# ScalarE's planes split first and its norms moved to the end of a convolution step, with a transposition issued ahead of weight loads

## The chip, the core and the metric

The kernel runs on one core of a Trainium2 chip. The metric is the device time of one execution in microseconds (us), the median of several runs. A core has five engines that run side by side and meet only at semaphores: TensorE (PE, matrix products), VectorE (DVE), ScalarE (ACT), GpSimd (POOL) and SyncE (SP), which here issues almost all DMAs.

## The reference

The program is two gated layers over x (8 batches, 256 rows, 512 columns) with a context of the same shape. The change touches only the first part of it:

```
x = x + tanh(g_xattn[0]) * _L0_xattn_ref(ctx, ctx, _layernorm(x), ssm_kernel, D, 8)
x = x + tanh(g_ffn[0])   * _L0_ffn_ref(_layernorm(x), w1, w2, w3)
x = x + tanh(g_xattn[1]) * _L1_xattn_ref(_layernorm(x), ctx, mask)
x = x + tanh(g_ffn[1])   * _L1_ffn_ref(_layernorm(x), w1, w2, w3)
```

`_L0_xattn_ref` takes, in each of 32 heads of 8 rows, all products of context row i with context row j, convolves each of them along the 512 columns with the head's own kernel (plus D times the product), multiplies with row i of the normed x and sums over i:

```
kv  = einsum('bhil,bhjl->bijhl', k, v)
out = irfft(rfft(kv) * rfft(ssm_kernel))[..., :L] + kv * D
out = einsum('bijhl,bhil->bjhl', out, q)        # q = layernorm(x)
```

## The kernel before

x lies in 16 tiles of 128 rows by 512 columns; a tile n holds two heads of all eight batches. The convolution runs in 16 steps, n = 0 to 15, each of two heads (hh = 0, 1). It is written as products with Toeplitz blocks. Every engine has its own loop over n, written out by hand, and the order inside a loop is the order of the code; nothing is planned by a scheduler. A step is made of these parts:

- GpSimd: `pairs(n + 1)` multiplies context rows (L583, L586); `finish_heads` closes the sum over i (L600, L603); `ln_root(n + 3)` and `conv_offset(n + 3)` make the scale and the offset of the norm of x's tile n + 3 from VectorE's sums (L296, L302, L591); `add_result(n - 2)` adds the finished step n - 2 to x (L607).
- TensorE: `conv_head(n, 0)` and `conv_head(n, 1)`, 36 float32 products each, 72 records in the trace (L740). Between the two stands `turn_result(n - 2)` (L732), which transposes a finished result into a PSUM bank. That bank is also one of the banks of `conv_head(n, 1)`. So in the middle of that head, after 21 of its 36 products, TensorE waits on `s_re`, for ScalarE to have copied the result away. `conv(n)` begins only when `pairs(n)` (`s_kv`), the squares (`s_sq`) and its Toeplitz block have come.
- VectorE: `products(n, hh)` reads the convolution from PSUM and multiplies it with the normed x (L1334, L1336, L1338, L1343), `fold_heads` (L1349) adds, `ln_sums(n + 3)` makes the sums of x's tile n + 3 (L287, L289).
- ScalarE: the path of the normed x, the squares of the context (`square`, L1097), the copy of the result (`copy_result(n - 2)`, L1114), and work on the first feed-forward's weights, `sum_weight` (L1118) and `ternary` (L1125, L1128).

The normed x has a path of its own from tile 2 on. `norm_q(n)` (L1105, two instructions) writes the normed tile into `xh_c`; it waits for GpSimd's offset (`s_off`). `split_q(n)` (L1070, two) takes the float32 words apart into two planes of 16-bit halves in `q_planes`. SyncE's `turn_q_planes(n)` (L378) is a DMA transposition of both planes into `qT_planes`. `join_q(n)` (L1081, four) puts the halves together again for VectorE. `q_planes` and `qT_planes` exist once: `split_q(n + 1)` waits until transposition n has landed, and transposition n + 1 waits until `join_q(n)` is done (`s_qc`) and `split_q(n + 1)` is done (`s_xh`).

SyncE's queue is one row of DMAs and waits in the order of the code: in a step x's tile n + 4, the context of step n + 2, weight chunks of the first feed-forward (two chunks of 704 KB in steps 0 to 3, one in steps 5 to 8; L384), the transposition, and the Toeplitz block of step n + 2 (L366). A wait holds all that stands behind it.

Of the kernel before, what the change touches and what calls it, by code (L numbers as in the profile page):

```python
# [24 lines left out]
def at(v, off, dims):  # L25
    return bass.AP(v.tensor, v.offset + off, [v.ap[0]] + dims)


def flamingo_two_layers(nc, xc, cx, ctxt_in, ctx_in, mask, g_xattn, g_ffn, taps_in, dskip, a_w, b_w, out):
    NT = xc.shape[0]  # L30
# [35 lines left out]
    with ExitStack() as ctx:  # L66
# [276 lines left out]
        def chunk_of(v, j, size):  # L343
            return v[:, j * size:(j + 1) * size]

        with nc.Block() as block:
            @block.sync
            def _(sp):
                def load_context(n):
                    if n >= 2:  # L350
                        sp.wait_ge(s_kv, n)
                        if n == 2:
                            sp.wait_ge(s_first, 3)
                        sp.wait_ge(s_sq, n)
                    sp.dma_start(cx_sb[n % 2], cx[n]).then_inc(s_cx[n % 2], 16)

                def load_x(n):
                    sp.dma_start(x_sb[:, n, :], xc[n]).then_inc(s_xl[n], 16)

                def load_toeplitz(n):  # L360
                    if n >= 2:
                        sp.wait_ge(s_y, 2 * n - 2)
                    if n == 2:
                        sp.wait_ge(s_kpad, 16)
                    rows = (kpad if n >= 2 else taps_in)[n * G:n * G + G, :]
                    sp.dma_start(toep[n % 2], bass.AP(rows.tensor, rows.offset, [[1, P], [TAP, G], [1, L]])  # L366
                                 ).then_inc(s_tp[n % 2], 16)
# [6 lines left out]
                def turn_q_planes(n):  # L374
                    sp.wait_ge(s_xt, 2 + 16 * (n - 2))
                    sp.wait_ge(s_xh, 2 * n)
                    sp.wait_ge(s_qc, n)
                    sp.dma_start_transpose(qT_planes, q_planes).then_inc(s_xt, 16)  # L378

                def load_weight(w, j):  # L380
                    if w == 2:
                        sp.wait_ge(s_wr, j + 1)
                        sp.wait_ge(s_ws, j + 1)
                    sp.dma_start(chunk_of(w_in[w % 2], j, AC), a_w[w][:, j * AC:(j + 1) * AC]).then_inc(s_w[w][j // 2], 16)  # L384

                def turn_x(t):
                    sp.wait_ge(f_qi, t + 1)
                    if t >= 4:
                        sp.wait_ge(f_up, 3 * (t - 4) + 3)
                    sp.dma_start_transpose(fa_qT[t % 4], fa_qi[t % 2]).then_inc(f_xT[t % 4], 16)  # L390
# [18 lines left out]
                def load_b(j):  # L409
                    home = B_HOME[j]  # L410
                    if j == 0:
                        sp.wait_ge(s_wr, 8)
                        sp.wait_ge(s_ws, 8)
                    if j == 5:
                        sp.wait_ge(s_xh, 2 * NT - 2)
                    if j == 6:
                        sp.wait_ge(s_rt, NT)
                        sp.wait_ge(s_prod, 2 * NT)
                    if home >= 8:
                        sp.wait_ge(c_m, NT)  # L420
                    elif home in B_HOME[:j]:
                        sp.wait_ge(s_ba, max(q for q in range(j) if B_HOME[q] == home) + 1)
                    sp.dma_start(b_in[home], b_w[j // PERW][:, (j % PERW) * BCH:(j % PERW + 1) * BCH]
                                 ).then_inc(s_b[home % 8], 16)
# [25 lines left out]
                for n in range(NT):  # L450
                    if n + 4 < NT:
                        load_x(n + 4)
                    if n + 2 < NT:
                        load_context(n + 2)
                    for w, first in ((0, 0), (1, 2)):
                        if n in (first, first + 1):
                            load_weight(w, 2 * (n - first))
                            load_weight(w, 2 * (n - first) + 1)
                    if 5 <= n < 9:
                        load_weight(2, n - 5)  # L460
                    if n == 0:
                        sp.wait_ge(s_dadd, 1)
                        sp.dma_start(kpad[:, :], kp_sb).then_inc(s_kpad, 16)
                    if n + 2 < NT:
                        turn_q_planes(n + 2)
                        load_toeplitz(n + 2)
                    if n in B_EARLY:
                        load_b(B_EARLY[n])
                    if n == 15:
                        sp.wait_ge(s_qc, NT)  # L470
                        sp.dma_start(mask_u8, mask.rearrange("b c -> (b c)").rearrange("(a n) -> a n", a=1)
                                     .to_broadcast([P, B * C])).then_inc(s_gate, 16)
                    if n >= NT - 2:
                        turn_x(n + 2 - NT)
# [579 lines left out]
            def _(act):  # L1054
# [9 lines left out]
                def split_q(n):  # L1064
                    act.wait_ge(s_xh, 2 * n - 1)
                    if n >= 3:
                        act.wait_ge(s_xt, 2 + 16 * (n - 2))
                    src = xh_c[n % 2].bitcast(U16)
                    for half in range(2):
                        last = nc.scalar.activation(q_planes[:, half * L:(half + 1) * L], at(src, half, [[2, L]]), ACT.Copy)  # L1070
                    last.then_inc(s_xh, 1)
# [28 lines left out]
                def norm_q(n):  # L1100
                    act.wait_ge(s_off, n + 1)
                    if 2 <= n < 4:
                        act.wait_ge(s_xt, n - 1)
                    for first, swap in ((0, Q), (P + Q, -Q)):
                        last = nc.scalar.activation(at(xh_c[n % 2], first - first % P, [[2 * P, 2], [Q, 2], [1, Q]]),  # L1105
                                                    at(x_sb[:, n, :], first, [[2 * P, 2], [swap, 2], [1, Q]]), ACT.Identity,
                                                    bias=ln_off[:, n:n + 1], scale=ln_rs[:, 0, n:n + 1])
                    last.then_inc(s_xh, 1)

                def copy_result(n, bk):  # L1110
                    act.wait_ge(s_rt, n + 1)
                    if n >= 2:
                        act.wait_ge(s_r0, n - 1)
                    nc.scalar.activation(rt[n % 2], bank(bk), ACT.Copy, scale=gates[:, 0:1]).then_inc(s_re, 1)  # L1114
# [6 lines left out]
                def ternary(w, j):  # L1121
                    if j == 0:
                        act.wait_ge(s_mean, 2 * w + 2)
                    src = chunk_of(w_in[w % 2], j, AC)
                    nc.scalar.activation(src, src, ACT.Identity, bias=magic[:, 0:1], scale=a_inv[:, w:w + 1]  # L1125
                                         ).then_inc(s_wr, 1)
                    act.wait_ge(s_wr, 4 * w + j + 1)
                    nc.scalar.activation(chunk_of(a_flat[w], j, AC), src, ACT.Sign, bias=magic[:, 1:2]).then_inc(s_ws, 1)  # L1128
# [83 lines left out]
                for n in range(NT):  # L1212
                    if n == 2:
                        act.wait_ge(s_kpad, 16)
                    if n == 0:
                        copy_q(1)
                    elif n + 1 < NT:
                        join_q(n + 1)
                    if n + 1 < NT:
                        square(n + 1)  # L1220
                    if n + 2 < NT:
                        norm_q(n + 2)
                        split_q(n + 2)
                    if n == 0:
                        act.wait_ge(s_gate, 32)
                        nc.scalar.activation(gates[:, :], gates[:, :], ACT.Tanh).then_inc(s_tanh, 1)
                        act.wait_ge(s_tanh, 1)
                        act.wait_ge(s_const, 6)
                    if n >= 2:
                        copy_result(n - 2, 4)  # L1230
                    for w in range(3):
                        for j in range(4):
                            if ABS_STEP[w, j] == n:
                                sum_weight(w, j)
                            if TERN_STEP[w, j] == n:
                                ternary(w, j)
                    if NT - 3 <= n < NT - 1:
                        a_round_x(n + 3 - NT)

# [520 lines left out]
```

## Time and profile before

| | us |
|---|---|
| median of 3 runs | 692.6 (692.45 to 693.28) |
| the profiled execution, its own time | 695.11 |
| its span in the trace | 693.3 |
| PE busy | 678.9 (98%) |
| DVE busy | 582.7 (84%) |
| ACT busy | 414.9 (60%) |
| POOL busy | 295.0 (43%) |

The convolution takes about the first 173 us of the span; then come the first feed-forward, the attention and the second feed-forward. In the chain of work that ended last, GpSimd holds 15% of the span, VectorE 6% and TensorE 68%. GpSimd's part lies in the convolution; from 178.87 us on the chain consists almost only of TensorE's products. Busy shares are averages over these stages, so a change in the convolution has to be read inside the convolution.

### The profile page before, as it was taken

The page shows a single profiled execution, that of the slowest core. Times are in us where ns is not written, and L with a number is a line of the kernel's source. Part 1 is how long each engine was busy: PE and PEld are TensorE (multiplying, and loading weights), DVE is VectorE, ACT ScalarE, POOL GpSimd, SP SyncE. Part 2 cuts the span into 40 slices and gives each one's busy share as a digit, 9 for nine tenths or more (in the row PEclk, how much of TensorE's full clock was granted, in tenths as well). Part 3 has the DMA queues.
Part 4 walks back from the last instruction along what each step waited for, and adds up shares of the span by engine and source line. Part 5 has one row for each costly group of instructions (what it writes and reads, how often), then busy time and mean ns, then how long its engine had stood idle before and what let it go on. Part 6 is the DMA issues. An engine that isn't in the chain of part 4 may idle for free.

```text
span 693.3 us, 12921 instructions
## 1 busy us (share of the span) xinstructions
PE 678.9 (98%) x4826; PEld 357.8 (52%) x4826; DVE 582.7 (84%) x1054; ACT 414.9 (60%) x646; POOL 295.0 (43%) x455
## 2 busy tenths in 40 slices
PE   9989999999999999999999999999999999999997
PEld 6756555555444444567754444444444444444445
DVE  5979999998998998658958889988888888898891
ACT  3689999856679989748667444434434434434440
POOL 6869999999765544537400521111110111110000
PEclk9999999999999999999999999999999999999999
DMA  8797775553379789998042243363332334342234
GB/s 296 222 293 209 227 188 141 148 148 111 102 167 194 187 167 201 218 357 308 17 136 17 61 94 75 91 92 92 76 90 41 68 92 92 77 78 59 61 71 112
DMA packets 155390, 94.85 MB, mean 137 GB/s; under 512 B 133825, under 2 KB 134337, under 8 KB 155329
## 3 DMA queue, kind: packets, MB, share of 16 engines
q1 hardware_dynamic: 153600, 90.02, 51.8%
q0 software_dynamic: 1200, 3.93, 1.7%
q8 instruction: 38, 0.62, 0.4%
q14 instruction: 24, 0.19, 0.1%
q10 hardware_dynamic: 528, 0.09, 0.1%
HBM read 53.04 MB, written 8.47 MB: 89 GB/s over the span
## 4 chain that ended last, share of the span: by engine, by line
PE 68%; POOL 15%; DVE 6%; issue 3%; ACT 2%; DMA 1%; SPq 0%; POOLq 0%; ACTq 0%
PE psum L955 29%; PE psum L987 15%; PE psum L882 9%; POOL phase_space L583 5%; PE psum L894 4%; PE psum L938 4%; PE psum L916 4%; POOL phase_space L600 3%; POOL x_sb L607 2%; POOL phase_space L586 2%; POOL phase_space L603 1%; PE psum L740 1%; PE psum L971 1%; DMA x_sb<-x_between 1%; POOL ln_rs L302 1%
## 5 line engine op out<-in xcount | busy, mean ns | idle before, releaser
L955 PE MATMUL psum<-phase_space 128*128 128x512 f16 x1024 | 223.8, 379 | 0.1
L955 PEld LDWEIGHTS psum<-phase_space 128*128 128x128 f16 x1024 | 100.0, 98 | 122.2 <-issue 1.7
L740 PE MATMUL psum<-phase_space 64*64 64x288 f32 x2304 | 150.3, 409 | 6.3 <-POOL phase_space L586 3.5
L740 PEld LDWEIGHTS psum<-phase_space 64*64 64x64 f32 x2304 | 89.9, 134 | 61.0 <-POOL phase_space L586 8.5
L712 POOL DMA_DIRECT2D out<-x_sb x15 | 9.3, 621 | 234.6 <-DVE x_sb L1516 234.6
L987 PE MATMUL psum<-phase_space 128*128 128x512 f16 x480 | 105.7, 379 | 0.0
L1281 ACT ACTIVATE phase_space<-psum,b_scalars 128x512 f32<-128x512 f32 x64 | 43.4, 682 | 75.2 <-PE psum L955 75.1
L1287 ACT ACTIVATE phase_space<-phase_space,magic 128x1024 f32<-128x1024 f32 x32 | 36.4, 1148 | 77.3 <-DVE phase_space L1500 77.3
L882 PE MATMUL psum<-phase_space 128*128 128x512 bf16 (+1 forms) x384 | 78.8, 361 | 0.7 <-DVE phase_space L1343 0.7
L987 PEld LDWEIGHTS psum<-phase_space 128*128 128x128 f16 x480 | 47.0, 98 | 56.6
L1485 DVE SCALAR_TENSOR_TENSOR phase_space<-psum,b_scalars,phase_space 128x512 f32<-128x512 f32 x64 | 47.7, 748 | 28.4 <-ACT phase_space L1281 28.3
L882 PEld LDWEIGHTS psum<-phase_space 128*128 128x128 bf16 x384 | 37.4, 98 | 40.9 <-issue 0.8
L583 POOL TENSOR_TENSOR phase_space<-phase_space 128x512 f32<-128x512 f32 x45 | 48.2, 1097 | 0.0
L1440 DVE TENSOR_REDUCE phase_space<-phase_space 128x8 f32<-128x512 f32 (+1 forms) x32 | 47.4, 1480 | 0.6
L287 DVE BATCH_NORM_STATS2 ln_bn<-x_sb 128x6 f32<-128x512 f32 x64 | 43.5, 680 | 3.0 <-DMA x_sb<-x_between 2.6
L1334 DVE TENSOR_TENSOR phase_space<-psum,phase_space 128x1024 f32<-128x1024 f32 x32 | 39.0, 1220 | 5.6 <-PE psum L740 4.9
L307 POOL TENSOR_SCALAR phase_space<-x_sb,ln_nm,ln_rs 128x512 f32<-128x512 f32 x48 | 38.0, 791 | 12.4 <-POOL ln_rs L302 5.8
L894 PE MATMUL psum<-phase_space 128*128 128x512 bf16 x176 | 40.6, 379 | 1.0 <-issue 0.6
L1147 ACT ACTIVATE phase_space<-psum,a_scalars 128x512 f32<-128x512 f32 (+1 forms) x48 | 30.8, 642 | 14.4 <-PE psum L882 13.1
L314 POOL TENSOR_TENSOR phase_space<-phase_space 128x512 f16<-128x512 f32 x12 | 13.8, 1179 | 59.4 <-ACT phase_space L1293 59.4
L1507 DVE SCALAR_TENSOR_TENSOR phase_space<-phase_space 128x1024 f32<-128x1024 f32 x32 | 37.8, 1223 | 1.3
L1382 DVE SCALAR_TENSOR_TENSOR phase_space<-psum,a_scalars,phase_space 128x512 f32<-128x512 f32 (+1 forms) x48 | 33.2, 696 | 5.9 <-ACT phase_space L1147 4.9
(123 smaller groups left out, 1081.7 us busy)
## 6 DMA issues: line engine op xcount, KB each, us to landing
phase_space<-in_L_weights SPq DMA_DIRECT2D x24, 512.0 KB, 6.0
phase_space<-in_L_weights SPq DMA_DIRECT2D x12, 704.0 KB, 7.1
phase_space<-kpad SPq DMA_DIRECT2D x14, 512.0 KB, 4.3
phase_space<-in_context_heads SPq DMA_DIRECT2D x15, 384.0 KB, 5.2
x_sb<-in_x_tiles SPq DMA_DIRECT2D x16, 256.0 KB, 4.8
phase_space<-in_context_turned SPq DMA_DIRECT2D x8, 512.0 KB, 5.9
x_between<-x_sb SPq DMA_DIRECT2D x16, 256.0 KB
x_sb<-x_between SPq DMA_DIRECT2D x16, 256.0 KB, 6.8
```

Source lines behind the costliest of these rows:

```text
L287: nc.vector.bn_stats(ln_bn[:, stage, n % 2, :], x_sb[:, n, :]).then_inc(s_ln[stage], 1)
L307: nc.gpsimd.tensor_scalar(dst, x_sb[:, n, :], ln_nm[:, stage, n:n + 1], ln_rs[:, stage, n:n + 1], ALU.add, ALU.mult).then_inc(s_done, 1)
L583: nc.gpsimd.tensor_tensor(at(kv_k, d * E, [[NP, rows], [1, E]]), at(cx_sb[k], 0, [[EX, rows], [1, E]]), at(cx_sb[k], d, [[EX, rows], [1, E ...
L740: return nc.tensor.matmul(at(dst, 0, [[64, B], [1, NP]]), toep[n % 2][row:row + Q, hh, shift:shift + Q], kv[n % 2][row:row + Q, IN_SLOT[j] ...
L882: last = nc.tensor.matmul(bank(UPA[c][part])[:, 0:w], fa_qT[t % 4][:, kk, :], a_wT[part][:, kk, c0:c0 + w], start=(kk == 0), stop=(kk == L ...
L894: last = nc.tensor.matmul(bank(6 + t % 2), fa_hT[t % 2][:, c, :], a_wT[2][:, c, :], start=(c == 0), stop=(c == JA - 1))
L955: last = nc.tensor.matmul(bank(2 * (m % 3) + w), fb_qT[n % 2][:, kk % 2, kk // 2, :], b_wT[w][:, kk // 2, c * 512:(c + 1) * 512], start=(k ...
L987: last = nc.tensor.matmul(bank(6 + k), fb_hT[k][:, part, c, :], b_wT[2][:, c, :], start=(c == 0 and part == 0), stop=(c == JB - 1 and part ...
L1281: nc.scalar.activation(fb_s[m % 2], bank(2 * (m % 3)), ACT.Silu, scale=fb_sm[:, n % 4, 2:3]).then_inc(g_si, 1)
L1334: nc.vector.tensor_tensor(at(pr, 0, [[SLOTS, rows], [E, 4], [1, E]]), at(y, 0, [[64, rows], [1, 32]]), at(q, 0, [[EX, rows], [1, 4], [1, E ...
L1440: nc.vector.tensor_reduce(gx[:, 0, :], grouped(src), AX.X, ALU.max, apply_absolute_value=True).then_inc(s_steps, 1)
L1485: nc.vector.scalar_tensor_tensor(fb_h[n % 2][:, c * 512:(c + 1) * 512], bank(2 * (m % 3) + 1), fb_sm[:, n % 4, 3:4], fb_s[m % 2], ALU.mult ...
```

## The change

ScalarE's step is put in another order. Before, in a step n it did `join_q(n + 1)`, `square(n + 1)`, `norm_q(n + 2)`, `split_q(n + 2)`, `copy_result(n - 2)`, and then the weights. Now it does `split_q(n + 2)`, `join_q(n + 1)`, `square(n + 1)`, `copy_result(n - 2)`, the weights, and `norm_q(n + 3)` last. Step 0 keeps its order and has `norm_q(3)` added at its end. SyncE issues the transposition of a step ahead of that step's weight chunks, from step 1 on, and no longer behind them.

```
@@ SyncE
                     if n + 2 < NT:
                         load_context(n + 2)
+                    if 1 <= n < NT - 2:
+                        turn_q_planes(n + 2)
                     for w, first in ((0, 0), (1, 2)):
                         if n in (first, first + 1):
                             load_weight(w, 2 * (n - first))
@@
                     if n == 0:
                         sp.wait_ge(s_dadd, 1)
                         sp.dma_start(kpad[:, :], kp_sb).then_inc(s_kpad, 16)
+                        turn_q_planes(2)
                     if n + 2 < NT:
-                        turn_q_planes(n + 2)
                         load_toeplitz(n + 2)
@@ ScalarE
                     if n == 2:
                         act.wait_ge(s_kpad, 16)
+                    if 1 <= n < NT - 2:
+                        split_q(n + 2)
                     if n == 0:
                         copy_q(1)
                     elif n + 1 < NT:
                         join_q(n + 1)
                     if n + 1 < NT:
                         square(n + 1)
-                    if n + 2 < NT:
-                        norm_q(n + 2)
-                        split_q(n + 2)
+                    if n == 0:
+                        norm_q(2)
+                        split_q(2)
@@
                             if TERN_STEP[w, j] == n:
                                 ternary(w, j)
+                    if n + 3 < NT:
+                        norm_q(n + 3)
                     if NT - 3 <= n < NT - 1:
                         a_round_x(n + 3 - NT)
```

No instruction is added or removed. In the changed file the lines of ScalarE stand two lines lower (L1105 is L1107, L1114 is L1116, and so on; the tanh of the gates, L1226, is L1230).

Here is ScalarE before, from the weight sums of step 1 (L1118) to the copy of the first result in step 2 (L1114):

```order
L1118 ACTIVATE phase_space,a_abs<-phase_space 128x1408 x2
L1081 ACTIVATE phase_space<-phase_space 128x64x8
L1081 ACTIVATE phase_space<-phase_space 128x64x4
L1081 ACTIVATE phase_space<-phase_space 128x64x8
L1081 ACTIVATE phase_space<-phase_space 128x64x4
L1097 ACTIVATE phase_space<-phase_space 128x64x8
L1105 ACTIVATE phase_space<-x_sb,ln_off,ln_rs 128x2x128 x2
L1070 ACTIVATE phase_space<-phase_space 128x512 x2
L1114 ACTIVATE phase_space<-psum,gates 128x512
```

And the same place of ScalarE now, from the weight sums of step 1 (L1120) to the same copy (L1116):

```order
L1120 ACTIVATE phase_space,a_abs<-phase_space 128x1408 x2
L1107 ACTIVATE phase_space<-x_sb,ln_off,ln_rs 128x2x128 x2
L1072 ACTIVATE phase_space<-phase_space 128x512 x2
L1083 ACTIVATE phase_space<-phase_space 128x64x8
L1083 ACTIVATE phase_space<-phase_space 128x64x4
L1083 ACTIVATE phase_space<-phase_space 128x64x8
L1083 ACTIVATE phase_space<-phase_space 128x64x4
L1099 ACTIVATE phase_space<-phase_space 128x64x8
L1116 ACTIVATE phase_space<-psum,gates 128x512
```

The norm and the split of tile 4 stood behind the join of tile 3 and the square; now they stand ahead of them. What stands between the weight sums and the copy is the same work.

On SyncE's queue this is the difference in step 1, with the transposition (L378), the two weight chunks (L384) and the Toeplitz block (L366):

```order
 L355 DMA phase_space<-in_context_heads 128x768
+L378 DMA_TRANSPOSE phase_space<-phase_space 128x8x128
 L384 DMA phase_space<-in_L_weights 128x1408 x2
-L378 DMA_TRANSPOSE phase_space<-phase_space 128x8x128
 L366 DMA phase_space<-kpad 128x2x512
```

The transposition has moved up past the two chunks, so the chunks now stand behind its waits. The Toeplitz block is behind all three, as it was.

## Rows read from the trace of the kernel before

**Rows 1.** Windows of 20 us: start:end, length, busy us and count per engine, clock, DMA.

```profile
20.00:40.00 20.00, 17.48 (x262) 12.21 (x258) 17.66 (x24) 14.55 (x26) 18.57 (x25) 0.94 0.98 294
...
100.00:120.00 20.00, 19.02 (x296) 11.24 (x292) 19.39 (x25) 18.91 (x28) 19.14 (x24) 1.00 0.56 142
```

**Rows 2.** Chain that ended last, whole span: start, us, engine and line.

```profile
38.20 7.99 PE psum L740 x102
...
55.66 3.57 POOL phase_space L583 x3
...
147.79 3.11 POOL phase_space L583 x3
```

**Rows 3.** Timeline of PE, convolution: start, us, line, count, [idle before, releaser].

```profile
15.69 16.31 PE L740 MATMUL psum<-phase_space 64*64 64x288 f32 x264
...
32.82 3.12 PE L740 MATMUL psum<-phase_space 64*64 64x288 f32 x42
38.20 7.99 PE L740 MATMUL psum<-phase_space 64*64 64x288 f32 x102 [2.26 <-ACT phase_space L1114]
...
160.84 6.69 PE L740 MATMUL psum<-phase_space 64*64 64x288 f32 x102 [0.52 <-ACT phase_space L1114]
```

**Rows 4.** Window of 2 us behind TensorE's long wait, columns as in rows 1.

```profile
38.00:40.00 2.00, 1.80 (x16) 1.05 (x20) 0.01 (x1) 2.00 (x4) 1.72 (x4) 0.50 1.18 374
```

**Rows 5.** Timelines of DVE and of POOL, steps 2 and 3.

```profile
41.89 1.22 DVE L1334 TENSOR_TENSOR phase_space<-psum,phase_space 128x1024 f32<-128x1024 f32 x1 [3.88 <-PE psum L740]
...
29.82 0.27 POOL L591 TENSOR_SCALAR ln_off<-ln_ag,ln_rs 128x1 f32<-128x1 f32 x1
...
47.25 0.73 POOL L603 TENSOR_TENSOR phase_space<-phase_space 128x256 f32<-128x256 f32 x1
51.76 0.19 POOL L296 TENSOR_SCALAR ln_ve<-ln_ag 128x1 f32<-128x1 f32 x1 [3.77 <-DVE ln_ag L289]
```

**Rows 6.** Timeline of ACT, from the first join to the first copy.

```profile
24.29 2.11 ACT L1081 ACTIVATE phase_space<-phase_space 128x512 uint16<-128x512 uint16 x4 [4.85 <-DMA phase_space<-phase_space]
26.26 0.61 ACT L1097 ACTIVATE phase_space<-phase_space 128x512 f32<-128x512 f32 x1
...
27.89 1.15 ACT L1070 ACTIVATE phase_space<-phase_space 128x512 uint16<-128x512 uint16 x2
...
32.85 2.08 ACT L1081 ACTIVATE phase_space<-phase_space 128x512 uint16<-128x512 uint16 x4 [1.10 <-issue]
...
37.48 0.67 ACT L1114 ACTIVATE phase_space<-psum,gates 128x512 f32<-128x512 f32 x1
```

**Rows 7.** Timeline of SP's queue, step 1: start of issue and its length.

```profile
23.61 0.90 SPq L384 DMA_DIRECT2D phase_space<-in_L_weights  x2
29.10 1.24 SPq L378 DMA_TRANSPOSE phase_space<-phase_space  x1
```

**Rows 8.** Transpositions (L378): those issued at 37.63, then at 57.80, to landing.

```profile
DMA to landing us min/median/max: 5.5/5.5/5.5
...
DMA to landing us min/median/max: 2.8/2.8/2.8
```

**Rows 9.** Weight chunks (L384), all twelve issues of the convolution, to landing.

```profile
DMA to landing us min/median/max: 5.1/7.1/9.9
```

**Rows 10.** Timelines of POOL, ACT, PE and DVE within one later step.

```profile
93.39 0.27 POOL L591 TENSOR_SCALAR ln_off<-ln_ag,ln_rs 128x1 f32<-128x1 f32 x1
...
102.66 0.19 POOL L296 TENSOR_SCALAR ln_ve<-ln_ag 128x1 f32<-128x1 f32 x1
...
93.69 1.09 ACT L1105 ACTIVATE phase_space<-x_sb,ln_off,ln_rs 128x256 f32<-128x256 f32 x2 [0.32 <-POOL ln_off L591]
...
96.03 4.59 PE L740 MATMUL psum<-phase_space 64*64 64x288 f32 x72
101.12 4.59 PE L740 MATMUL psum<-phase_space 64*64 64x288 f32 x72 [0.49 <-POOL phase_space L586]
...
101.22 1.23 DVE L1334 TENSOR_TENSOR phase_space<-psum,phase_space 128x1024 f32<-128x1024 f32 x1
```

More of the change, by code:

```diff
@@ L454, in _ @@
                         load_context(n + 2)
+                    if 1 <= n < NT - 2:
+                        turn_q_planes(n + 2)
                     for w, first in ((0, 0), (1, 2)):
@@ L463, in _ @@
                         sp.dma_start(kpad[:, :], kp_sb).then_inc(s_kpad, 16)
+                        turn_q_planes(2)
                     if n + 2 < NT:
-                        turn_q_planes(n + 2)
                         load_toeplitz(n + 2)
@@ L1214, in _ @@
                         act.wait_ge(s_kpad, 16)
+                    if 1 <= n < NT - 2:
+                        split_q(n + 2)
                     if n == 0:
@@ L1220, in _ @@
                         square(n + 1)
-                    if n + 2 < NT:
-                        norm_q(n + 2)
-                        split_q(n + 2)
+                    if n == 0:
+                        norm_q(2)
+                        split_q(2)
                     if n == 0:
@@ L1236, in _ @@
                                 ternary(w, j)
+                    if n + 3 < NT:
+                        norm_q(n + 3)
                     if NT - 3 <= n < NT - 1:
```

## The prediction, made before the changed kernel was run

> **What bounds the kernel now.** I read the chain of waits first, since busy shares mix the stages. Inside the convolution it has two parts. Up to 55.66 us it passes from ScalarE to TensorE, VectorE and GpSimd; from there on it is GpSimd alone, step after step [rows 2]. `pairs` starts at 55.66 and, nine steps later, at 147.79: 10.24 us a step. The windows agree: between 100 and 120 us GpSimd is busy 19.14 of 20 us [rows 1]. So from 55.66 us on a change on ScalarE gains nothing unless it changes GpSimd's start; it can only lose something by making GpSimd wait. What can be gained lies ahead of 55.66.
>
> There TensorE's timeline shows the place [rows 3]. In step 2 it does 42 records of `conv_head(2, 1)` from 32.82 on, then sits idle for 2.26 us and resumes at 38.20, released by ScalarE's L1114, which is `copy_result(0)`. That wait costs more than itself. The 102 records behind it take 7.99 us; the same 102 behind a short wait of 0.52 us at 160.84 take 6.69 us [rows 3]. The granted clock is 0.50 between 38 and 40 us, the lower of its two levels (1.2 and not 2.4 GHz), after the idle stretch [rows 4]. VectorE then waits 3.88 us for TensorE, and GpSimd 3.77 us for VectorE's sums of x at 51.76, though its work of that time had ended at 47.98 [rows 5]. All behind that is GpSimd's chain.
>
> **The change part by part.** No instruction comes or goes, so the sum is of times at which `copy_result(0)` ends, and what follows from it. I follow ScalarE from the row at 24.29, where it begins on transposition 2, which landed then [rows 6]. Nothing ahead of that moves but `norm_q(3)`, which goes into step 0: it takes 1.12 us (1.09 of one pair and the gap to the next [rows 10]) and falls in the 4.85 us in which ScalarE waits for that transposition [rows 6].
>
> - `split_q(3)`, now first: 24.29 to 25.35 (1.06 us from a split's start to the next start, 27.89 to 28.95 [rows 6]).
> - `join_q(2)`: 1.97 us (24.29 to 26.26 [rows 6]), to 27.32. `square(2)`: 0.61, ending at 27.93, the next start at 27.83.
> - Transposition 3 may be issued when both are done, at 27.4 instead of 29.10 [rows 7].
> - The two weight sums of step 1: 2.80 us (28.95 to 31.75, where the idle time of the row at 32.85 begins [rows 6]), to 30.63. `norm_q(4)`: its offset is there at 30.09 [rows 5]; to 31.75.
> - `split_q(4)` needs transposition 3 landed. Transpositions took 2.8 and 5.5 us at the ends [rows 8], so it lands between 30.2 and 32.9. I take 3.7, what it took in this place before (29.10 to about 32.8, where ScalarE takes it up [rows 6, 7]): 31.1, before ScalarE needs it. `split_q(4)` to 32.81, `join_q(3)` to 34.76, `square(3)` to 35.27, `copy_result(0)` to 35.94, against 37.48 + 0.67 = 38.15 [rows 6].
>
> The transposition's late end, 5.5 us, would put all this 1.15 us later. It took 5.5 us at 37.63, with weight chunks issued shortly ahead of it, and 2.8 us at 57.80, where the step had no chunks [rows 8]; now no chunk of its own step stands ahead of it. The Trainium skill (DMA: Bandwidth & Descriptors, "Queues, rings and completion order") says that each DMA engine takes up the descriptors of a ring in their order, so what is issued later queues behind. Those two rows agree with it; by that rule the transposition lands near the short end and the 1.15 us are not paid, and the chunks pay instead. Without it the late end stays in my range.
>
> TensorE pays something back in step 2. It ran without a gap from 15.69, 264 records in 16.31 us [rows 3]; of these 48 and 144 belong to steps 0 and 1, so `conv(2)` began at 15.69 + 192 x 0.0618 = 27.56, and it needs `square(2)`, now done at 27.93 and not at 26.87: 0.4 us late. Half of it is lost in the short wait ahead of `turn_result(0)`; the 42 records then end 0.2 us later. At full clock they take 42 x 0.0639 = 2.68 us, so TensorE comes to its wait at 32.82 + 2.68 + 0.2 = 35.7 and resumes at 36.0: a wait of 0.3 us instead of a long one.
>
> The sum: TensorE resumes 38.20 - 36.0 = 2.2 us earlier, and the 102 records behind it take 7.99 - 6.69 = 1.3 us less, at the clock of rows 3. Together 3.5 us. VectorE takes it all, being free at 41.89 - 3.88 = 38.0, about when the head is done. GpSimd's L296 was ready at 47.98; it would start at 51.76 - 3.5 = 48.3 and still waits, so the 3.5 us pass to it whole. The most it could take is 3.77 [rows 5], and 0.6 us more from a wait on VectorE's fold just ahead, as it then starts the step earlier: 4.4 in all.
>
> Does it arrive at the end? From 55.66 on GpSimd's work is unchanged, and 52.2 is where it starts now. The next test is ScalarE in the later steps, where the new order puts `copy_result` behind more work. `norm_q` starts at 93.69, right after GpSimd's offset [rows 10]; now split, join, square and copy follow it, 1.12 + 1.06 + 1.93 + 0.51 + 0.67 = 5.29 us, so the copy ends at 98.98. TensorE wants it after 42 records, at 96.03 + 2.68 = 98.71, and is 0.3 us late in every such step. But it waits 0.49 us for `pairs` at the next step's start anyway [rows 10]: the 0.3 us come out of that. VectorE needs that head at 101.22, and gets it at 100.6 + 0.3. Cost nothing. If that cover were gone, the cost would be 0.3 us in each of some eight steps, 2.4 us. `square` is done at 98.3, ahead of 101.12. The last three steps have ScalarE waiting for VectorE, and take up what is late.
>
> The weight chunks of step 1 move from 23.61 [rows 7] behind the transposition, to about 28.7 and 29.2. They land 5.1 to 9.9 us later [rows 9]; 7.1 gives 36.3. ScalarE wants them at 35.9, and `norm_q(5)` behind them waits for GpSimd until 39.3 anyway. Their sums are done near 39.2, and VectorE needs the total at about 41.6. Cost nothing; beyond a landing at 38.2 they would delay `copy_result(1)`, which TensorE wants at 46.3. The chunks of later steps have a step or more to spare, and the Toeplitz blocks keep their place, since they wait for the convolution's end.
>
> The profiled execution took 695.11 us, with 1.8 us around its span; it would be 691.6. It lies 2.5 above the median, and the 3.5 us are a difference inside it, so from the median: 692.6 - 3.5 = 689.1.
>
> **The rivals.**
>
> A, partial gain: the chunks or the transposition land late. A chunk landing 9.9 us after 29.2 comes at 39.1, `copy_result(1)` ends at 47.2, TensorE waits 0.9 us in step 3: gain 2.6, time 690.0. The transposition at its 5.5 us: the copy ends at 37.1, the wait is 1.4 us, gain 1.1 to 2.4 depending on the clock, 690.2 to 691.5. For it: the DMA share of 0.98 between 20 and 40 us [rows 1]. Against it: both would have to come at or near the longest row.
>
> B, nothing to be measured: the wait shrinks but the clock falls all the same, and the transposition is late too. Gain 1.1 or less, 691.5 to 692.6. Against it: the clock stayed up behind the 0.52 us wait [rows 3].
>
> C, slower: in steps 6 to 13 TensorE now has a wait inside a head, on `copy_result`. If that second gap a step brought the clock down, the 102 records behind would take 1.3 us more, of which 0.2 are covered by what is left of the 0.49: 1.1 in eight steps, 8.8 us, less the 3.5 gained: 697.9. It decides from five such steps on. Against it: TensorE idles no more per step than now, and the window from 100 to 120 us, with a gap of 0.49 a step, has a clock of 1.00 [rows 1, 10]. And a late head alone, with no fall of the clock, reaches GpSimd only over VectorE's sums, which end at 101.3 and are wanted at 102.66 [rows 10]: another 1.3 us to spare.
>
> D, the change does not do what it says: `norm_q(n + 3)` waits for its offset and holds the split, join and square behind it, so the transposition loop runs no earlier. In later steps this is so; there it does not matter. In steps 1 and 2 the offset is there before ScalarE is (30.09 against 30.63). This would give 692.6.
>
> **How the numbers follow.** The forecast 689.1 (gain 3 to 4.4) has a chance of 0.73, A 0.13, B and D together 0.08, C 0.06. What can be told from no change is about 0.2%, 1.4 us. Faster by more: the forecast and A, 0.86; within: 0.08; slower: 0.06. The low end is the most GpSimd can take, 4.4: 688.2. The high end is A's, 691.3; beyond both lie B, D and C.
>
> **What would show it.** Right: TensorE's wait on L1116 in step 2 is under 0.6 us and the clock stays at 1.00 from 34 to 44 us; GpSimd's wait at L296 in step 3 falls from 3.77 to about 0.5 to 1 us (it starts at 48.3); `pairs` starts at 52.2 and again every 10.2 us; in later steps TensorE has small waits on L1116, and those on GpSimd shrink by as much. Wrong: ScalarE's L1072 in step 2 waits for the transposition past 32 us, its L1120 waits for chunks past 38 us, or the step grows beyond 10.24 us, with the clock below 1.00 in 60 to 150 us.

## The result, and the profile after

| | us |
|---|---|
| before, median of 20 runs | 693.12 (692.45 to 693.8) |
| changed, median of 20 runs | 691.48 (691.02 to 692.42) |
| ratio | 0.9977, 95% interval 0.9971 to 0.9984 |
| the profiled executions, before and changed | 695.11 and 691.55 |
| their spans | 693.3 and 689.7 |

The change gains 1.6 us; 3.5 were forecast. Single runs over 1.5% above the fastest of their kernel (two of before and one of a variant, all in the comparisons below) are in no median. The two profiled executions, though, differ by 3.6 us (691.6 was forecast for that of the changed kernel), and their rows differ as the prediction said. This is TensorE's timeline of the changed kernel in steps 2 and 3:

```profile
15.68 11.94 PE L742 MATMUL psum<-phase_space 64*64 64x288 f32 x192
27.89 4.59 PE L742 MATMUL psum<-phase_space 64*64 64x288 f32 x72 [0.27 <-ACT phase_space L1099]
...
33.00 3.12 PE L742 MATMUL psum<-phase_space 64*64 64x288 f32 x42
36.30 6.53 PE L742 MATMUL psum<-phase_space 64*64 64x288 f32 x102 [0.18 <-ACT phase_space L1116]
```

The wait on the copy is 0.18 us where [rows 3] have 2.26, and the 102 records behind it take 6.53 us, not 7.99. `conv(2)` now waits 0.27 us for `square(2)`, which was foreseen. The granted clock in windows of 2 us (columns as in rows 1) stays up where [rows 4] have 0.50:

```profile
36.00:38.00 2.00, 1.82 (x29) 1.13 (x32) 1.93 (x4) 2.00 (x4) 1.73 (x2) 1.00 1.07 382
38.00:40.00 2.00, 2.00 (x39) 1.24 (x34) 1.53 (x3) 1.61 (x4) 1.68 (x4) 1.00 1.09 324
```

GpSimd's timeline, step 3 and the start of step 4, against [rows 2, 5]: its wait for VectorE's sums is 0.38 us and not 3.77, and `pairs` starts at 52.43, 3.2 us earlier.

```profile
48.54 0.19 POOL L296 TENSOR_SCALAR ln_ve<-ln_ag 128x1 f32<-128x1 f32 x1 [0.38 <-DVE ln_ag L289]
...
52.43 3.57 POOL L585 TENSOR_TENSOR phase_space<-phase_space 128x512 f32<-128x512 f32 x3
```

From 62.96 on the chain of waits (start, us, what) has GpSimd's `pairs` once a step, every 10.2 us, as before:

```profile
62.96 3.11 POOL phase_space L585 x3
...
93.54 3.12 POOL phase_space L585 x3
103.73 3.12 POOL phase_space L585 x3
```

So the mechanism is in the profile, and yet half of the time is missing in the median. The place to look is the kernel before.

### The profile page after: what moved, and what is told of

Same layout as the page of the kernel before. It is cut to its first block, busy times and chain, and to the rows that moved or that the text cites. A ratio compares the mean times of both kernels' runs of the same rounds, so it can differ in the third digit from the quotient of the medians.

```text
span 689.7 us, 12909 instructions
## 1 busy us (share of the span) xinstructions
PE 680.3 (99%) x4814; PEld 359.3 (52%) x4826; DVE 582.2 (84%) x1054; ACT 414.2 (60%) x646; POOL 295.1 (43%) x455
## 4 chain that ended last, share of the span: by engine, by line
PE 73%; POOL 15%; DVE 5%; ACT 3%; issue 2%; DMA 2%; POOLq 0%; ACTq 0%; SPq 0%
PE psum L957 29%; PE psum L989 15%; PE psum L884 11%; PE psum L896 5%; POOL phase_space L585 5%; PE psum L940 4%; PE psum L918 4%; POOL phase_space L602 3%; POOL x_sb L609 2%; DMA phase_space<-phase_space 2%; PE psum L742 2%; POOL phase_space L588 2%; POOL phase_space L605 1%; PE psum L973 1%; PE psum L907 1%
## 5 line engine op out<-in xcount | busy, mean ns | idle before, releaser
L742 PE MATMUL psum<-phase_space 64*64 64x288 f32 x2304 | 152.6, 407 | 1.0 <-ACT phase_space L1116 0.6
L742 PEld LDWEIGHTS psum<-phase_space 64*64 64x64 f32 x2304 | 91.4, 133 | 56.5 <-ACT phase_space L1116 4.5
```

Source lines behind the costliest of these rows:

```text
L742: return nc.tensor.matmul(at(dst, 0, [[64, B], [1, NP]]), toep[n % 2][row:row + Q, hh, shift:shift + Q], kv[n % 2][row:row + Q, IN_SLOT[j] ...
```

## Experiments

All ratios are to the kernel before on the same chip, with 95% intervals. Lines of the changed kernel are two higher than those of before. "`pairs` of step 4" is what GpSimd does in its own step 4.

### The kernel before, once more

No edit.

> The kernel before once more, for a second profile and the granted clock of each timed run. The question: the profiled executions differ by 3.6 us (695.11 and 691.55), the medians by 1.64 us (693.12 and 691.48). Theory 1 (the profiled execution of before was not typical: TensorE's wait in step 2 was long enough there to bring the clock down, in most executions it is not, or less so): ratio to before 1.000, the new profiled time lies near 693.1, its wait on L1114 in step 2 is under 2.26 us or its 102 records take less than 7.99 us, and the mean clock of most timed runs is above the 0.997 of that profile. Rival (the wait and the fall of the clock are the same in every execution, and the changed kernel loses some 2 us elsewhere that its profile does not show): the wait is again about 2.26 us, 7.99 us behind it, and the clock of most runs is 0.997.

Measured: ratio 0.9999 (0.999 to 1.0008), median 693.31, profiled execution 692.89 with a span of 691.0. Its TensorE timeline at the same place, and a window of 2 us behind the wait:

```profile
32.82 3.12 PE L740 MATMUL psum<-phase_space 64*64 64x288 f32 x42
37.67 6.53 PE L740 MATMUL psum<-phase_space 64*64 64x288 f32 x102 [1.73 <-ACT phase_space L1114]
```

```profile
38.00:40.00 2.00, 2.00 (x40) 1.28 (x36) 0.11 (x1) 2.00 (x3) 1.73 (x4) 1.00 1.08 280
```

The same program waits 1.73 us here, not 2.26, resumes 0.53 us earlier, and its clock does not fall: 6.53 us for the 102 records. The first join of ScalarE starts 0.54 us earlier, since transposition 2 was issued 0.23 us earlier and landed 4.5 and not 4.8 us after its issue:

```profile
23.75 2.10 ACT L1081 ACTIVATE phase_space<-phase_space 128x512 uint16<-128x512 uint16 x4 [4.54 <-DMA phase_space<-phase_space]
```

Both together are 2.0 us at the end of the 102 records (46.19 against 44.20), of 2.3 us between the two spans. GpSimd's wait on VectorE in step 3 is 2.0 us. Against this profile the changed kernel is 1.37 us earlier at TensorE's resumption (37.67 to 36.30), and its span is 1.3 us shorter: near the measured gain. Theory 1 holds, by this one further profile and by the times of the other runs. That the clock of most runs would lie above 0.997 was right too: the runs list 0.998 to 1.000. A mean of 0.998 or 0.999 is no sign of a fall in step 2, though: in this profile the mean is 0.999 with a clock of 1.00 in step 2, because it is lower at the very end (0.82 from 688 to 690 us, 0.50 behind that), where TensorE has no work left.

Timed runs like the first profile exist, but are few: of 98 runs of before in all comparisons, 9 took 693.9 us or more, up to 695.2. Five of them, at 694.6 to 695.2, have a mean clock of 0.996 to 0.998, as a fall would leave it; the other four, at 693.9 to 694.5, have 1.000 and so no such fall. Of 31 runs of the changed kernel none took more than 692.42. That the clock fell in step 2 in those five is inferred from their time and mean; only profiles show the place.

### Each half alone

SyncE's half, ScalarE as before:

```
+                    if 1 <= n < NT - 2:
+                        turn_q_planes(n + 2)   # ahead of load_weight
...
```

> SyncE's part of the change alone: the transposition issued ahead of the weight chunks, ScalarE in its old order. Transposition 3 still waits for split_q(3), so it is issued near 29.1; ahead of it no chunk of its step. My theory (ScalarE's order is what brings the copy forward): the transposition lands up to 0.9 us earlier, so the wait of 2.26 us shrinks by 0 to 0.9; gain over before 0 to 0.9 us, ratio 0.9987 to 1.000. Rival (the chunks on the queue are what makes it late): the gain is most of the whole change's 1.6 us, ratio 0.9977.

Measured: 0.9989 (0.998 to 0.9998), 692.61 us. ScalarE's half, SyncE as before:

```
+                    if 1 <= n < NT - 2:
+                        split_q(n + 2)         # ahead of join_q(n + 1)
...
+                    if n + 3 < NT:
+                        norm_q(n + 3)          # at the step's end
```

> ScalarE's part of the change alone: split first, norm of the next but one last; SyncE in its old order. My theory: transposition 3 is issued near 27.4 behind chunks that were issued at 23.6; even if it takes 4.8 us it lands at 32.2, so the copy of the first result ends within about 0.5 us of where it ends in the whole change: gain 1.2 to 1.6 us, ratio 0.9977 to 0.9983. Rival (both parts are needed): under half of it, ratio above 0.9988.

Measured: 0.9989 (0.998 to 0.9998), 692.50 us. TensorE's timeline at the place in question, of SyncE's half and then of ScalarE's half:

```profile
37.20 6.53 PE L742 MATMUL psum<-phase_space 64*64 64x288 f32 x102 [1.10 <-ACT phase_space L1116]
```

```profile
36.57 6.53 PE L740 MATMUL psum<-phase_space 64*64 64x288 f32 x102 [0.52 <-ACT phase_space L1114]
```

Against 37.67, SyncE's half resumes 0.47 us earlier and ScalarE's 1.10, where the whole change has 1.37. These three differences are not the edits' alone, since transposition 2, ahead of all that was moved, landed at another time in each profile. ScalarE's first instruction behind it starts at 24.29 and 23.75 us in the two profiles of before, at 23.43 in SyncE's half, 23.41 in ScalarE's half, and 24.16 and 23.69 in the two of the changed kernel. From there to the start of `copy_result(0)` it is 13.2 us in both profiles of before, 13.05 in SyncE's half, 12.44 in ScalarE's half, and 11.4 and 11.2 in the changed kernel. Counted so, SyncE's half brings 0.15 us alone, ScalarE's 0.8, and both together 1.8 to 2.0, more than the sum. What ScalarE's half lacks is in its row of `split_q(4)`, where ScalarE waits for transposition 3:

```profile
32.33 1.15 ACT L1070 ACTIVATE phase_space<-phase_space 128x512 uint16<-128x512 uint16 x2 [1.01 <-DMA phase_space<-phase_space]
```

It was issued at 26.63 us, behind the chunks, and took 5.6 us. In the changed kernel, with the same order on ScalarE and the chunks behind it, it took 4.6 and 4.3, and 2.8 to 4.6 in the four profiles of kernels built on it. In the medians each half gains 0.7 to 0.8 us of the 1.6, with intervals of 0.6 us to each side that do not tell them apart. SyncE's half is where I expected it; ScalarE's half fell short of my 1.2 to 1.6 us, and its 0.9989 is at the rival's edge. So ScalarE's order is what brings the copy forward, and by these profiles it needs SyncE's to bring all of it.

### One copy moved, all else as before

```
+                    if n == 2:
+                        copy_result(0, 4)      # behind square(3), ahead of norm_q(4)
...
-                    if n >= 2:
+                    if n >= 3:
                         copy_result(n - 2, 4)
```

> The kernel before with one thing moved: in step 2 alone, copy_result(0) stands directly behind square(3), ahead of norm_q(4) and split_q(4). The copy then ends near 36.0 instead of 38.15, all else on ScalarE and SyncE as before. My theory (the whole gain is TensorE's wait for this one copy): the same time as the changed kernel, ratio to before 0.9970 to 0.9983, and GpSimd's pairs of step 4 start near 52.4. Rival (the gain comes from the earlier transpositions in all steps): ratio 0.999 to 1.000.

Measured: 0.9983 (0.9975 to 0.9992), 692.42 us. TensorE's timeline:

```profile
33.02 8.96 PE L740 MATMUL psum<-phase_space 64*64 64x288 f32 x144
...
42.72 3.12 PE L740 MATMUL psum<-phase_space 64*64 64x288 f32 x42
46.69 6.53 PE L740 MATMUL psum<-phase_space 64*64 64x288 f32 x102 [0.86 <-ACT phase_space L1114]
```

The wait in step 2 is gone, but one of 0.86 us has come up in step 3, on `copy_result(1)`: that copy again stands behind a norm and a split, and these behind a join that waits for its transposition. GpSimd starts `pairs` of step 4 at 52.37, as foreseen and as early as the changed kernel, but that of step 8 at 94.17, where the changed kernel has it at 93.54, and it stays 0.6 to 0.7 us behind. The medians give 0.9 us of the 1.6. So one moved copy explains a good half of the gain, and not all of it as my theory had it. That the wait in step 3 costs the rest fits the rows; no run takes it away alone.

### The wait put back into the changed kernel, by two lengths

No edit, for the reference:

> The changed kernel once more, beside the three that are built on it, on one chip. It gives their reference and a second profile. Theory 1 says that its wait in step 2 is short in every execution and never brings the clock down: ratio to before 0.997 to 0.998, TensorE resumes near 36.3, and its times spread less upwards than those of before (of some 50 executions of before 6 took 693.9 us or more).

Measured: 0.998 (0.9971 to 0.9989), 691.78 us (691.37 to 692.06), `pairs` of step 4 at 52.64; the ratio and the small spread are as expected. Its TensorE shows no gap of its own in step 2, a row of 144 records in 9.25 us from 32.93 on.

```
-                    if n >= 2:
+                    if n >= 3:
                         copy_result(n - 2, 4)
...
                                 sum_weight(w, j)
+                                if (w, j) == (0, 2):
+                                    copy_result(0, 4)
```

> The changed kernel with copy_result(0) put behind one of the two weight sums of step 2, so that it ends 1.36 us later. TensorE's wait becomes about 1.6 us, near the 1.73 us of the second profile of before. My theory (a wait of this length costs its own length and leaves the clock up in most executions): pairs of step 4 start near 53.7, the time is 1.2 to 1.4 us above the changed kernel's, so about that of the kernel before, ratio 0.9995 to 1.000. Rival (what the change gains is the earlier norm and transposition in the later steps): within 0.5 us of the changed kernel.

Measured: 0.9999 (0.999 to 1.0008), 692.73 us, 0.95 above the reference: the ratio is as expected, the difference is under my 1.2 to 1.4 us and over the rival's 0.5. Two of its eleven runs took 694.65 and 695.55, both with a mean clock of 0.998. With `(0, 3)` in the place of `(0, 2)`:

> The same with copy_result(0) behind both weight sums of step 2: it ends 2.7 us later than in the changed kernel, and TensorE's wait becomes about 2.9 us, longer than the 2.26 us of the first profile of before. My theory (a wait of this length brings the clock down in most executions and then costs 1.3 to 1.5 us more): 3.8 to 4.3 us above the changed kernel, ratio to before about 1.0035, the 102 records behind the wait take about 8 us. Rival (the fall of the clock had to do with that one execution, not with the length of the wait): 2.7 us above the changed kernel, ratio 1.0015 to 1.002, the 102 records take 6.5 us.

Measured: 1.0025 (1.0013 to 1.0037), 695.10 us, 3.3 above the reference. TensorE's timeline, of the first and then of the second, with GpSimd's `pairs` of step 4:

```profile
37.19 6.53 PE L742 MATMUL psum<-phase_space 64*64 64x288 f32 x102 [0.96 <-ACT phase_space L1116]
...
53.47 3.58 POOL L585 TENSOR_TENSOR phase_space<-phase_space 128x512 f32<-128x512 f32 x3
```

```profile
38.49 8.22 PE L742 MATMUL psum<-phase_space 64*64 64x288 f32 x102 [2.33 <-ACT phase_space L1116]
...
56.18 3.57 POOL L585 TENSOR_TENSOR phase_space<-phase_space 128x512 f32<-128x512 f32 x3
```

The waits are 0.96 and 2.33 us, not the 1.6 and 2.9 that I had expected: in the reference the copy ends at 35.59 us, some 0.5 us before TensorE wants it (3.12 us for 42 records from 32.93), and so much of the delay costs nothing. The first costs 0.83 us at `pairs` and 0.95 in the median, while the copy starts 1.5 us later (36.46 and not 34.93). The second splits its runs in two: four at 693.67 to 694.31 with a clock of 1.000, and six at 695.08 to 697.16 with 0.994 to 0.998. In the profile, one of the six, the clock is at the lower level after the wait. It is still up when TensorE resumes and falls about a microsecond later:

```profile
38.00:40.00 2.00, 1.51 (x20) 0.93 (x24) 0.20 (x2) 0.89 (x2) 1.49 (x4) 0.87 1.07 345
40.00:42.00 2.00, 2.00 (x24) 1.10 (x20) 0.26 (x1) 1.97 (x5) 1.92 (x3) 0.50 0.95 381
```

So the clock falls in some runs of one program and not in others. By the times it fell in two runs of eleven with one sum ahead of the copy and in six of ten with two. That it falls more often behind a longer wait is not shown: the counts are small, and before, whose wait is longer than that of the first program, has five such runs in 98. Without the fall the second program is 2.0 us above the reference (median of its four, 693.74), with it 3.8 (median of its six, 695.57): a fall costs some 1.8 us there (8.22 - 6.53 = 1.7 us in the 102 records), and 7.99 - 6.53 = 1.5 us between the two profiles of before. My "in most executions" holds by six runs of ten, my ratio of 1.0035 does not: for that every run would have had to fall.

### GpSimd's step made shorter

VectorE adds the epsilon, and L296 leaves GpSimd's step (the other stages keep it):

```
+            if stage == 0:
+                dve.wait_ge(s_ln[0], 3 * n + 2)
+                nc.vector.tensor_scalar(ln_ve[:, 0, n:n + 1], ln_ag[:, 0, n, 1:2], LN_EPS, 1.0,
+                                        ALU.add, ALU.mult).then_inc(s_ln[0], 1)
...
-            pool.wait_ge(s_ln[stage], 2 * n + 2)
-            nc.gpsimd.tensor_scalar(ln_ve[:, stage, n:n + 1], ...)
+            pool.wait_ge(s_ln[stage], 3 * n + 3 if stage == 0 else 2 * n + 2)
+            if stage > 0:
+                nc.gpsimd.tensor_scalar(ln_ve[:, stage, n:n + 1], ...)
```

On the changed kernel:

> The changed kernel with 0.28 us of work taken off GpSimd in each step of the convolution: VectorE adds the epsilon to the variance (some 0.15 us behind L289), GpSimd's L296 goes. My theory (from 63 us on GpSimd alone sets the step of 10.2 us, TensorE and VectorE could do 9.5 to 9.9): the distance of pairs falls from 10.19 to about 9.92 us from step 5 to 13, the time by 1.5 to 2.5 us, ratio to before 0.994 to 0.9955. Rival (TensorE's waits on the copy and VectorE's own work are as binding as GpSimd now): the distance stays above 10.1, the time within 0.7 us of the changed kernel.

Measured: 0.9924 (0.9912 to 0.9937), 687.90 us, 3.9 us under the reference. The chain of waits shows `pairs`:

```profile
81.76 3.57 POOL phase_space L592 x3
91.56 3.57 POOL phase_space L592 x3
101.35 3.58 POOL phase_space L592 x3
```

That is 9.8 us a step, 0.4 us less, not 0.28: with L296 (0.19 us) both gaps around it went (92.38 to 92.46 and 92.65 to 92.73 in the trace of before). Nine such steps are 3.6 us, so the gain is over my 1.5 to 2.5. The step became shorter by all that was taken off GpSimd, though VectorE has more to do: GpSimd alone sets it, and the rival is out. The same edit on the kernel before:

> The kernel before, in its old order on ScalarE and SyncE, with the epsilon added on VectorE. If GpSimd sets the step from about 55 us on and the change of order acts only ahead of it (my theory), the two gains add: pairs start near 53.7 in step 4 and come every 9.8 us behind that, the time is 3.3 to 3.9 us under that of before, ratio 0.9945 to 0.9952. Rival (with the old order ScalarE, with its join, norm and split behind each other, becomes the bound when GpSimd is faster): the distance of pairs stays above 10 us, the gain is under 2 us.

Measured: 0.9955 (0.9942 to 0.9967), 689.97 us, 3.0 us under before and so a little less than expected. And the one above again beside it:

> The changed kernel with the epsilon on VectorE once more, on the same chip as the one above, since it had five timed runs only. Expected 687.5 to 688.3 us, 1.2 to 2.2 us under the kernel above if the two gains add; more than 2.5 us under it if the new order on ScalarE is what lets the faster step come about.

Measured: 0.9923 (0.991 to 0.9937), 687.55 us, 2.4 under. Timelines of GpSimd in step 4, before with the edit and changed with the edit:

```profile
53.27 3.56 POOL L590 TENSOR_TENSOR phase_space<-phase_space 128x512 f32<-128x512 f32 x3
```

```profile
51.77 3.56 POOL L592 TENSOR_TENSOR phase_space<-phase_space 128x512 f32<-128x512 f32 x3
```

They are 1.5 us apart there and 2.1 from step 5 on (63.61 and 61.55), since GpSimd waits 0.50 us for VectorE in step 4 of the old order. Behind that both run at 9.8 us a step (the last `pairs` start at 152.95 and 150.81). So the old order does not hold the faster step up, and the gains add or do slightly better than that; 2.4 us between medians of five runs each, between my two cases, is not told apart from the 1.6 of the change alone. The changed kernel with the epsilon on VectorE is the fastest here, 5.4 us under the kernel before.

## Why the prediction was wrong, point by point

- **Where the kernel is bound**: right. From step 4 or 5 on GpSimd alone sets the step, shown by taking 0.4 us from it. The path of the gain (copy, TensorE, VectorE, GpSimd) is right too: in the pair of profiles it was read for, `pairs` of step 4 starts 3.2 us earlier.
- **The step that failed**: "so from the median: 692.6 - 3.5 = 689.1". Every term of the 3.5 us was read from one execution that took 695.11 us, 2.5 above the median. I noted that and took the difference as lying outside the place in question. It lay in it: the second profile has a wait of 1.73 and not 2.26 us, and 6.53 and not 7.99 us behind it. Of the terms, "102 records take 1.3 us less" is 0 in the second profile and, by the times, in most runs, and "resumes 2.2 us earlier" is 1.4. The sum by the second profile is 1.4 us; 1.6 were measured. The bound falls with it: "the most it could take is 3.77" is a wait of 2.02 us in the second profile.
- **TensorE's arrival** at its wait was put at 35.7, from 2.68 us for the 42 records. The row has 3.12 us, and the idle time of 2.26 counts from its end, 35.94; the changed kernel arrives at 36.12. It cost the forecast almost nothing, since the copy ended at 36.24.
- **ScalarE's times**: right but for one. `copy_result(0)` was to end at 35.94. The row of the changed kernel's ScalarE is

```profile
35.57 0.67 ACT L1116 ACTIVATE phase_space<-psum,gates 128x512 f32<-128x512 f32 x1
```

  an end at 36.24. The 0.3 us are transposition 3, which landed 4.6 us after its issue and not 3.7, so that ScalarE waited:

```profile
32.07 1.15 ACT L1072 ACTIVATE phase_space<-phase_space 128x512 uint16<-128x512 uint16 x2 [0.57 <-DMA phase_space<-phase_space]
```

  In its second profile it landed after 4.3 us, ScalarE did not wait, and the copy ended at 35.59.

- **The transposition ahead of its step's chunks**: my reading of the two extreme rows, and of the Trainium skill's rule (DMA: Bandwidth & Descriptors, "Queues, rings and completion order") that a ring's descriptors are taken up in order, was that it would land faster. Transposition 3 of the changed kernel took 4.6 and 4.3 us, and the next one 5.3 and 4.2, where before had 3.7 and 3.7, 5.5 and 5.4. That does not speak against the rule, since before issued transposition 3 later, at 29.10 and 28.54 us and 5.5 us behind its chunks. The nearer comparison is ScalarE's half, issued at 26.63 and 3.7 us behind them: 5.6 us, with a DMA share of 1.05 from 26 to 28 us, where the two profiles of the changed kernel have 0.13 and 0.00. There the rule agrees, by one profile of the half. For the next transposition it shows nothing (4.0 us in ScalarE's half). What else was in flight is not separated here.
- **The later steps**: right. The view lists no wait on GpSimd at the start of a head any more (3.5 us in eight of them before). The small waits on the copy that I had forecast do not show as rows of their own either, but two heads and what is between them take 9.68 us (from 92.77), as they did with a wait of 0.49 (from 96.03). The step is unchanged and the clock is 1.00 from 60 to 160 us, so rival C is out, and D, since the transpositions of steps 1 and 2 ran earlier. B is out too: the clock did not fall behind the short wait. The chunks cost nothing: the sums of step 2 begin at 36.14, without a wait.
- **Rival A** came near the time (690.0 to 691.5), but not by its mechanism: a late transposition made 0.3 us of the shortfall in one profile and none in the other. That 691.48 lies within its numbers is luck. The range ended at 691.3, under A's own 691.5, and I drew no bound from the 2.5 us between profile and median.

## What to carry to other kernels

Before a gain is read out of one profiled execution, its own time has to be held against the median. Where it lies above by as much as the gain that is hoped for, the wait in question may be longer there than in most runs, and a second profile of the same program can show it. Here an idle stretch of TensorE of some 2 us cost its own length in most runs and 1.5 to 1.8 us more in some, so removing it also narrowed the spread. Profiles are compared from the last event that neither edit moves, here the landing of transposition 2, and not from the start of the span. And where one engine worked without a gap through a stage, moving a 0.2 us instruction off it was worth more than all reordering ahead of it.

## What the runs showed that I had not expected

- Whether TensorE's clock falls behind a wait is not the same from run to run of one program: behind 1.73 us it did not fall in the second profile, behind 2.26 and 2.33 us it did, and with two sums ahead of the copy four runs of ten kept a mean clock of 1.000.
- The landing of transposition 3 hardly follows its issue. In eleven of the twelve profiles it was issued between 26.63 and 29.10 us, took 5.6 us at the early end and 3.6 or 3.7 at the late end, and landed between 31.2 and 32.8. It is no rule: in the twelfth, of the fastest kernel, it was issued at 26.65 and took 2.8 us. Of the 1.8 to 2.0 us that ScalarE gains between transposition 2 and the copy, 1.1 are the norm that is now done while transposition 2 is on its way; most of the rest is the shorter wait for transposition 3 (1.10 and 1.13 us before, 0.57 and none now).
- A GpSimd instruction of 0.19 us on one column takes 0.4 us of a full step together with the gaps around it.
